# Both value waves of a quad in one slot of the 16-wide attention

## What is computed

```python
q = (xn @ Wq.T + bq); k = (ctx @ Wk.T + bk); v = (ctx @ Wv.T + bv)   # layer 3: no biases, v is k
score = einsum('bldn,bmdn->blmn', q, k) / 4          # 16 heads, 16 dimensions
x = x + softmax(score, over m) @ v @ Wo.T + bo
```

## Time and profile before

| | us |
|---|---|
| median of 3 runs | 3937.5 |
| lowest and highest of them | 3936.36, 3937.7 |
| the profiled execution | 3933.27 |
| its span (first to last instruction) | 3931.3 |
| mean granted TensorE clock | 0.87 of full |

### The profile page before, as it was taken

One profiled execution on the slowest core, in us unless ns is written; L12 is line 12 of the kernel. 1 busy time (PEld: TensorE's weight loads), 2 busy tenths in 40 slices (PEclk: granted clock), 3 DMA queues, 4 the chain that ended last, 5 costly groups with the idle time before them and its releaser, 6 DMA issues. The chain is left out here.

```text
span 3931.3 us, 51885 instructions
## 1 busy us (share of the span) xinstructions
PE 3037.3 (77%) x18878; PEld 2095.6 (53%) x18894; DVE 2030.1 (52%) x4388; ACT 1209.8 (31%) x2434; POOL 748.2 (19%) x628
## 2 busy tenths in 40 slices
PE   2999955568886669999999964459999608999990
PEld 1555523346664446666666643335555507788780
DVE  3677759945553345555555558946666311111113
ACT  0444435522222214333333333414444201111110
POOL 0455520000000001111111110025444150000006
PEclk8999989967775789999999977779999658999995
DMA  5565550010000010000000000055654121212214
GB/s 126 101 120 103 114 174 0 0 29 22 21 22 4 0 53 6 4 6 6 6 6 4 4 25 0 3 110 107 120 102 87 47 80 38 78 55 70 68 35 128
DMA packets 186889, 204.82 MB, mean 52 GB/s; under 512 B 41008, under 2 KB 162512, under 8 KB 186704
## 3 DMA queue, kind: packets, MB, share of 16 engines
q1 hardware_dynamic: 180560, 185.53, 20.0%
q0 software_dynamic: 6144, 16.79, 1.3%
HBM read 141.97 MB, written 60.29 MB: 51 GB/s over the span
## 5 line engine op out<-in xcount | busy, mean ns | idle before, releaser
L1442 POOL TENSOR_TENSOR L2x_halves_sum<-L2x_probs 128x512 f32<-128x512 f32 x128 | 163.0, 1274 | 1602.9 <-ACT L2x_probs L1456 1602.9
L3353 PE MATMUL L3f_pY<-L3f_W,L3f_hT 128*128 128x256 f32 x1184 | 272.0, 390 | 0.0
L3345 PE MATMUL L3f_pH<-L3f_xgT,L3f_W 128*128 128x256 f32 x1184 | 264.3, 382 | 0.8 <-ACT L3f_xgT L3364 0.8
L1137 DVE TENSOR_REDUCE L3x_mx<-L3x_pS 128x2 f32<-128x512 f32 x256 | 170.9, 687 | 154.3 <-PE L3x_pS L1258 154.0
L3353 PEld LDWEIGHTS L3f_pY<-L3f_W,L3f_hT 128*128 128x128 f32 x1184 | 230.0, 197 | 31.6
L3345 PEld LDWEIGHTS L3f_pH<-L3f_xgT,L3f_W 128*128 128x128 f32 x1184 | 226.8, 192 | 32.5 <-issue 1.2
L1137 DVE TENSOR_REDUCE L0x_mx<-L0x_pS 128x2 f32<-128x512 f32 x256 | 170.8, 687 | 134.2 <-PE L0x_pS L1258 134.0
L1023 ACT ACTIVATE L3x_probs<-L3x_pT 128x512 f32<-128x512 f32 x256 | 151.4, 597 | 264.1 <-PE L3x_pT L1274 263.7
L1023 ACT ACTIVATE L0x_probs<-L0x_pT 128x512 f32<-128x512 f32 x256 | 151.0, 599 | 252.3 <-PE L0x_pT L1274 252.0
L1000 POOL TENSOR_TENSOR L3x_halves<-L3x_probs 128x512 f32<-128x512 f32 x128 | 164.8, 1288 | 254.5 <-ACT L3x_probs L1023 253.7
L1000 POOL TENSOR_TENSOR L0x_halves<-L0x_probs 128x512 f32<-128x512 f32 x128 | 164.2, 1288 | 228.8 <-ACT L0x_probs L1023 228.1
(11 more groups left out here) (549 smaller groups left out, 6769.9 us busy)
## 6 DMA issues: line engine op xcount, KB each, us to landing
L0x_k_stack<-L0x_k_parts_dram SPq DMA_DIRECT2D x128, 128.0 KB, 4.6
L3x_k_stack<-L3x_k_parts_dram SPq DMA_DIRECT2D x128, 128.0 KB, 4.8
L3f_W<-in_L3f_W SPq DMA_DIRECT2D x16, 1024.0 KB, 7.6
L0x_q_stack<-L0x_q_parts_dram SPq DMA_DIRECT2D x32, 384.0 KB, 5.9
L3x_q_stack<-L3x_q_parts_dram SPq DMA_DIRECT2D x32, 384.0 KB, 6.0
tokens_by_expert<-zero_row SPq DMA_DIRECT2D x1, 10496.0 KB, 35.7
L3f_xg<-tokens_by_expert SPq DMA_DIRECT2D x38, 256.0 KB, 2.7
expert_outputs<-L3f_y SPq DMA_DIRECT2D x37, 256.0 KB, 2.2
```

What stands on the lines that cost most here:

```text
L1137: nc.vector.tensor_reduce(mx[:, :, i], pS[n % 2][:, :].rearrange("p (j s) -> p j s", j=TB), AX.X, ALU.max).then_inc(max_done, 1)
L1442: nc.gpsimd.tensor_tensor(halves_sum[n % 2][:, :, :], probs[n % 2][:, :, 0, :], probs[n % 2][:, :, 1, :], ALU.add).then_inc(halved, 1)
L3345: ins = nc.tensor.matmul(pH[c % 4][:, 0:TILE], W1[par][:, kc, c * P:(c + 1) * P], xgT[:, kc, :], start=kc == 0, stop=kc == KC - 1)
L3353: ins = nc.tensor.matmul(pY[j][:, 0:D], hT[:, c, j * P:(j + 1) * P], W2[par][:, c, :], start=c == 0, stop=c == HCH - 1)
```

## The change

In the program of TensorE the second value wave of each quad moves from its own slot into the slot of the first, right behind it. The sums stay where they were, two slots after. Which slot of the three has what:

| slot (of quad 3, 0, 1, 2) | before | after |
|---|---|---|
| 1, 5, 9, 13 | value wave kt=0 | value waves kt=0, kt=1 |
| 2, 6, 10, 14 | value wave kt=1 | none |
| 3, 7, 11, 15 | sums | sums |

The function also stands behind `wide_attention` in the file now, otherwise unchanged, so that its lines have other numbers (392 more). No other engine's program changes: VectorE, ScalarE, GpSimd and SyncE have the same instructions in the same order, with the same waits.

```diff
                     at = H * r + h - 5
                     if 0 <= at < H * B:
-                        if at % 4 < TB:
-                            times_v(at // H, at % H // 4, at % 4)
-                        elif at % 4 == TB:
+                        if at % 4 == 0:
+                            for kt in range(TB):
+                                times_v(at // H, at % H // 4, kt)
+                        elif at % 4 == 2:
                             sums(at // H, at % H // 4)
```

690 lines of the change are left out of this document (345 added, 345 removed).

## The result

The changed kernel took 3972.15 us (median of 6 runs, 3963.95 to 3980.3), the kernel before on the same chip 3936.93 (6 runs, 3931.02 to 3945.52): **35 us slower, ratio 1.0097, 95% interval 1.0078 to 1.0116.** The forecast was +10.5 us and its range ended at 3961: the direction was right, the size was not. The profiled execution took 3974.71 us, its span is 3972.8.

The account below looks back on a forecast made before the run. The prediction took the loop through slot 2's score, k's parts, save and stack loads to bound most rounds. Stack-ended rounds +9.0, TensorE-ended +0.8, rounds 14 and 15 -1.0, clock +1.7: +10.5 us, 3948 for the median, range 3938 to 3961.

Parts of the forecast that it names:

- What bounds the round: Round start, slots 0 and 1, score of slot 2, k's parts, save, loads, next start; slots 4 to 15 excluded.
- The pair's price: Two adjacent value waves on TensorE take 1.07 us; the second costs 0.43, and a pair saves 0.23 us.
- The maximum of slot 2, k's parts and the save of k move by the full 0.43: VectorE waits idle for slot 2's score, so its work and k's save come 0.43 us later each round.
- the latter doesn't lead: Slots 2 and 3: exponentials and the q side come 0.23 us earlier, but q's save follows the k loads.
- 21 rounds: Rounds of L0x and L3x that end when the stacks land: 0.43 us longer each, together +9.0 us.
- their +0.15 each: Five rounds of L0x and L3x ending with TensorE don't gain: between -0.1 and +0.43 us each, together +0.8.
- I take one more: Round starts: longer waits for stacks make one further round start at half TensorE clock, +1.7 us.
- The rival: Round starts: four to twelve more rounds begin at 1.2 GHz after longer waits, 3953 to 3966 us; chance 0.20.
- Slot 8, +0.20: The pair in slots 5 and 6 delays the divide and slot 7's maxima, so slot 8 starts 0.20 us later.
- The sum: All terms over L0x and L3x together: +10.5 us, 3948 us for the median.
- TensorE's saving: Rounds end with TensorE's own program, so 29.0 us go, or half of it: 3908.5 us; chance 0.09.
- the DMA engines take up the delay: Between k's save and round start, later loads run denser; a round loses 0 to 0.17 us, 3937 to 3941; chance 0.19.

Follow-up runs that it names:

- the halve kept back: Changed kernel plus a GpSimd wait holding the halving of heads 2 and 3 until VectorE has all k parts: 3939.06 us, +11 us against the kernel before.
- the second execution: The unmodified changed kernel measured and profiled again in a later group beside the kernel before: 3952.85 us, +31 us.
- the second slot's -25: All pairs of value waves in slots 2, 6, 10, 14 instead of the first slots: 3903.02 us, 25 us faster than the kernel before.
- quad 3 alone: Only quad 3 paired, in slot 1, quads 0 to 2 as in the kernel before: 3958.84 us, +31 us against that kernel.
- its control: Kernel before plus the GpSimd wait that holds the halving of heads 2 and 3 behind k's parts: 3928.68 us, ratio 1.0002.

## Why the forecast was right in its direction and wrong in its size

- **What bounds the round:** right. The loop through the score of slot 2, k's parts and the stacks sets it; moving VectorE's steps alone gave 23 us, and TensorE's shorter program gave nothing as long as the pair stood in that loop.
- **The pair's price:** right. 1.07 us, the score of slot 2 at 6.10, score_T at 6.32, the save in L0x at 10.01.
- **"The maximum of slot 2, k's parts and the save of k move by the full 0.43":** the term that was mis-sized. In L0x it is 0.43, in L3x 1.41: 12.9 us more over its 13 rounds, and most of the further half-clock starts with it. With the halve kept back 20 to 24 us went. The forecast took as fixed a duration (0.69 us) that depends on which of two engines starts first. The Trainium skill (SBUF — State Buffer, Who interferes with whom) says that a VectorE instruction with two inputs from this memory and a GpSimd instruction that reads it exclude each other, and that the one issued first keeps the ports for its whole length. The rows above agree with it, from both sides: 1.67 for 0.69 and 1.33 for 0.43 us where the halve was first, 1.48 for 1.27 where the step was. The lengths are some 0.15 us short of a full wait behind the other (2888.25 + 0.69 = 2888.94 for an end at 2888.79). The trace of before had the warning. In one of the first rounds of L3x, from 2619.38, the order was the other one already:

```profile
2628.93 1.27 POOL L1000 TENSOR_TENSOR L3x_halves<-L3x_probs 128x512 f32<-128x512 f32 x1 [2.59 <-ACT L3x_probs L1023]
2629.07 1.68 DVE L1117 TENSOR_TENSOR L3x_k_parts<-L3x_k_rest,L3x_k_parts 128x512 bf16<-128x512 f32 x1
```

  The prediction had both shifts, 0.43 later for k and 0.23 earlier for the exponentials, wrote that the latter doesn't lead, and never set one against the other.
- **21 rounds:** too few. In the profiled execution the five others end with the stacks too, so their +0.15 each should have been as large as the rest. In the second execution two of the 12 of L0x still ended without a wait.
- **"I take one more" half-clock start:** seven instead of three in the 13 rounds of L3x, and one of the 12 of L0x; five in L3x in the second execution, none in L0x. The rival had the mechanism and its price, but not the cause: the waits grew by 1 us and more through the held step, not by 0.3.
- **Slot 8, +0.20:** right in L3x, where its score starts 15.93 us after the round's start (2893.81 - 2877.88) for 15.74 before (2864.73 - 2848.99). In L0x it starts at 16.17 for 16.19. There the divide begins 0.19 later, but its second step, which GpSimd's last step on q holds up already in the kernel before, takes 0.81 us for 1.02 (first before, then after):

```profile
427.02 1.16 POOL L983 TENSOR_TENSOR L0x_q_parts<-L0x_q_rest,L0x_q_parts 128x512 bf16<-128x512 f32 x1
427.44 1.02 DVE L1158 SCALAR_TENSOR_TENSOR L0x_ln_sum<-L0x_ln_sum,L0x_inv 128x256 f32<-128x256 f32 x1
...
436.30 1.17 POOL L1375 TENSOR_TENSOR L0x_q_parts<-L0x_q_rest,L0x_q_parts 128x512 bf16<-128x512 f32 x1
436.94 0.81 DVE L1550 SCALAR_TENSOR_TENSOR L0x_ln_sum<-L0x_ln_sum,L0x_inv 128x256 f32<-128x256 f32 x1
```

  With only quads 0 to 2 paired the halve gets ahead of that step in L3x, which turns into a wait of 1.79 us and costs the kernel 28 us. The prediction saw none of these.
- **The sum:** with the halve kept back the changed kernel is at +11 (+8 to +19), for a forecast of +10.5. That is partly luck: the interval is wide, and the mean way from save to start in L0x was 19.16 us in one execution of the changed kernel and 18.43 in another.
- **The other rivals:** TensorE's saving did not count: in the changed kernel the rounds end with the stacks. That the second slot's -25 is near the 29.0 of that rival is no support for it, since there, too, nearly all rounds end with the stacks and most of the gain is the earlier save. That the DMA engines take up the delay isn't borne out: in L0x the mean way from k's save to the next start was 19.16, 18.43, 18.59 and 18.75 us in the four executions with a pair in slot 1 named above and the save at 10.01 (changed kernel twice, quad 3 alone, halve kept back), and 18.80 and 18.94 in those of before and of its control. It varies by more than the 0.43 in question, so a small part taken up can't be excluded.

## What to carry to other kernels

Where a round ends with a transfer, follow the loop back to the instruction that feeds it and keep added work out from in front of it: the same pairs of waves were worth +31 to +35 us ahead of that score and -25 us behind it. When a change moves one engine's work later and another's earlier, list the VectorE and GpSimd instructions that stand within a microsecond of each other, with the margin between them; if the two shifts together exceed it, the order flips and one has to wait for most of what is left of the other. And read a stage's odd rounds: a duration that is twice its usual value in one of them is the price of an order that the change may make the usual one.

## What the runs showed of the hardware

- A VectorE step of 128x512 with two inputs in the on-chip memory took 0.69 us alone and 1.67 when it came 0.14 us after the start of a GpSimd addition of 1.27 us; one of 128x256 took 0.43 and, 0.21 us after such a start, 1.33.
- The length of a wait alone doesn't decide on the clock behind it. After 3.08 and 2.63 us TensorE came back at 1.2 GHz, after 3.12 and 2.12 at 2.4. After 3.70 it came back at 2.4 and fell to 1.2 within slot 0: the fill of k took 3.48 us there instead of 1.89. What does decide was not found out.
- A stage can lock into a pattern in which every round pays both the held step and the half clock (ten rounds of 30.71 to 30.73 us), and is rid of it with one semaphore wait on another engine (28.4 us a round).
